# A four-layer graph network on one core: row sums of squares on ScalarE, a third layer with one scale, and another order of loads and of the first product

## The reference

```
x = LN(x + y / max(|y|, 1e-12)),   y = (adj @ x + x) @ w0 + b0
x = LN(x + softmax_like(8 tanh(QK'/ (8 sqrt(128)))) masked by adj, @ x @ v)
x = LN(x + (((si + sj + adj * w_r + g_b) @ x) @ w2 + b2))
x = LN(x + relu(x @ W0 + L x @ W1 + (2 L L - I) x @ W2 + b3))
LN(x) = (x - mean) / sqrt(var + 1e-5)
L = I - dis[:, None] * adj * dis[None, :],   dis = rowsum(adj) ** -0.5
```

## Time and profile before

| | us |
|---|---|
| median of 3 runs (728.14 to 728.96) | 728.53 |
| the profiled execution | 728.63 |
| its span, first to last instruction | 726.5 |
| TensorE busy | 645.3 (89%) |
| VectorE busy | 616.1 (85%) |
| ScalarE busy | 383.5 (53%) |
| GpSimd busy | 72.3 (10%) |

### The profile page before, as it was taken

The page is one execution under the profiler, slowest core; times in us unless marked ns, Lnnn a source line. Parts: engine busy times, 40 slices in busy tenths (PEclk is TensorE's granted clock), DMA queues, the critical chain, the costliest instruction groups (busy, mean ns, idle before and its releaser), DMA issues. The chain is left out here.

```text
span 726.5 us, 17484 instructions
## 1 busy us (share of the span) xinstructions
PE 645.3 (89%) x7478; PEld 488.2 (67%) x7478; DVE 616.1 (85%) x1562; ACT 383.5 (53%) x525; POOL 72.3 (10%) x49
## 2 busy tenths in 40 slices
PE   4937955889999999999999999999999999869894
PEld 3533633456886688667866687668866786638894
DVE  3789898998999899898989899989989897879525
ACT  3928914782359244944467255924494447613402
POOL 0020001000200111002200120011100220020002
PEclk9978996999999999999999999999999999989998
DMA  7100001000100020000200020002000010000102
GB/s 263 45 29 1 1 1 30 0 2 1 31 3 1 2 60 2 1 3 1 60 1 2 1 60 2 1 2 60 2 1 2 5 27 2 1 1 2 31 2 59
DMA packets 20013, 14.54 MB, mean 20 GB/s; under 512 B 864, under 2 KB 18912, under 8 KB 19936
## 3 DMA queue, kind: packets, MB, share of 16 engines
q1 hardware_dynamic: 18816, 12.91, 5.8%
q10 hardware_dynamic: 1120, 0.52, 0.3%
HBM read 9.24 MB, written 4.19 MB: 18 GB/s over the span
## 5 line engine op out<-in xcount | busy, mean ns | idle before, releaser
L240 POOL TENSOR_TENSOR small<-small,minus_half 128x8 f32<-128x8 f32 x39 | 67.9, 1745 | 602.7 <-DVE small L528 479.5
L1215 PE MATMUL av<-vhi,p_hi 128*128 128x129 f16 x512 | 90.1, 221 | 8.8 <-DVE p_lo L776 8.5
L375 ACT ACTIVATE att<-r,coef 128x1024 f32<-128x1024 f32 x64 | 70.4, 1100 | 49.8 <-PE r L1102 49.2
L1218 PE MATMUL av<-vhs,p_lo 128*128 128x129 f16 x512 | 89.9, 220 | 0.0
L1217 PE MATMUL av<-vlo,p_hi 128*128 128x128 f16 x512 | 89.8, 219 | 0.0
L771 DVE TENSOR_TENSOR att<-att,adjT 128x1024 f32<-128x1024 f32 x64 | 78.1, 1221 | 10.9 <-ACT att L377 10.9
L776 DVE SCALAR_TENSOR_TENSOR p_lo<-p_hi,att 128x1024 f16<-128x1024 f16 x64 | 78.1, 1221 | 0.0
L1100 PE MATMUL r<-gr,lap 128*128 128x128 f16 x448 | 75.8, 219 | 0.0
L1102 PE MATMUL r<-gr,lap 128*128 128x128 f16 x448 | 75.8, 219 | 0.0
L1101 PE MATMUL r<-gr,lap 128*128 128x128 f16 x448 | 75.8, 219 | 0.0
L1102 PE MATMUL r<-xq,lap 128*128 128x128 f16 x448 | 75.4, 219 | 0.0
(11 more groups left out here) (300 smaller groups left out, 1924.6 us busy)
## 6 DMA issues: line engine op xcount, KB each, us to landing
x<-in_x SPq DMA_DIRECT2D x8, 512.0 KB, 4.3
lap<-in_adj SPq DMA_DIRECT2D x8, 512.0 KB, 9.4
out<-outb SPq DMA_DIRECT2D x7, 512.0 KB, 3.4
out<-att SPq DMA_DIRECT2D x1, 384.0 KB, 2.8
b_bc<-in_L_gnn_bias SPq DMA_DIRECT2D x3, 64.0 KB, 7.2
x<-in_L_gnn_weight ACTq DMA_DIRECT2D x1, 192.0 KB, 8.1
out<-att SPq DMA_DIRECT2D x1, 128.0 KB, 2.7
x<-in_L_gnn_q ACTq DMA_DIRECT2D x1, 64.0 KB, 3.5
```

Of the source, the lines that this page charges most:

```text
L240: return nc.gpsimd.tensor_tensor(dst, src, minus_half[:], ALU.pow)
L375: nc.scalar.activation(att[:, s], (r1, r0)[t % 2][:], ACT.Tanh, scale=c_tanh).then_inc(S["th"], 1)
L1215: mm(acc, p_hi[:, s, chunk(j)], vhi[:, t, 0:D + 1], start=(t == 0 and j % 3 == 0), stop=False, skip_group_check=True)
L1218: l_ = mm(acc, p_lo[:, s, chunk(j)], vhs[:, t, 0:D + 1], start=False, stop=(t == C - 1), skip_group_check=True)
```

## The change

Row squares: the BATCH_NORM_STATS2 of y and the three operations that combined them are gone. ScalarE runs `row_squares(b, h)`, four Square activations with an accumulator for each half, into the same small tile. In the steady tail half 0 stands behind `y0_half(1)` and ahead of `x3t_hi`, half 1 between `r_hi` and `p_copy`; in steps -1 and 0 both follow `y0_half(1)`.

Third layer: the normalisation of x3 now includes the root of the degree, so the Laplacian of the scaled rows needs only one scale a row, -1/degree. The identity is no longer added: the weights are combined otherwise (w0+w1+w2, w1+4*w2 in place of w1, and w2). The broadcast of dis, its sixteen matmuls and `lap_row` are gone; both parts of a row come straight from adjT, all high parts from ScalarE in the tails of steps -1 and 0, low parts in the attention of steps 0 and 1. The bias is multiplied by the root of the degree (`bias_rows`), and the last normalisation's epsilon by the degree. Scale constants change with it.

`ln_arg` has five operations (norms 0 and 1) or six (2 and 3) in place of seven.

Loads: all of adj ahead of the broadcasts. Opening: y0 is made in eight blocks of 128 columns (`adj_x0_chunk`), one behind the transposes of the next adj block; VectorE makes the adjT copy of blocks 0 and 1; the low part of block 7 is made from PSUM; the first half is projected ahead of the last block; the scales of the weights come in pieces (`weights_max`, `weights_scale`, `weights_split`, `gate_weights`). All row sums of adj follow the squares on ScalarE, and GpSimd takes the row norms' root ahead of the degrees'.

```diff
-LN_ARG = 5
-LN_LINKS = 6
+LN_ARG = (4, 4, 5, 4)
+LN_LINKS = (5, 5, 6, 5)
+DVE_COPIES = 2
...
             for c in range(C):
                 sp.dma_start(adj_rows[:, c, :], adj_v[c]).then_inc(adj_in[c], 16)
-                if c == 1:
-                    for dst, src in ((b0_bc[:], b0), (b2_bc[:], b2), (b3_bc[:], b3.rearrange("a b d -> (a b d)")),
-                                     (wj_bc[:], gw[0:D]), (wi_bc[:], gw[D:2 * D]),
-                                     (wr_gb[:, 0:1], gw[2 * D:2 * D + 1]), (wr_gb[:, 1:2], gb)):
-                        sp.dma_start(dst, src.partition_broadcast(P)).then_inc(S["w_in"], 16)
+            for dst, src in ((b0_bc[:], b0), (b2_bc[:], b2), (b3_bc[:], b3.rearrange("a b d -> (a b d)")),
+                             (wj_bc[:], gw[0:D]), (wi_bc[:], gw[D:2 * D]),
+                             (wr_gb[:, 0:1], gw[2 * D:2 * D + 1]), (wr_gb[:, 1:2], gb)):
+                sp.dma_start(dst, src.partition_broadcast(P)).then_inc(S["bc_in"], 16)
...
+                if nxt:
+                    pool.wait_ge(S["e0_c"], 4 * (i + 2))
+                    inverse_root(small[:, 4, ROOT], small[:, 4, ARG]).then_inc(S["norm_r"], 1)
                 if is_first(i, -1):
                     pool.wait_ge(S["deg_ok"], C)
                     inverse_root(dis[:], deg[:]).then_inc(S["dis_ok"], 1)
-                if nxt:
-                    pool.wait_ge(S["e0_c"], 8 * (i + 2))
-                    inverse_root(small[:, 4, ROOT], small[:, 4, ARG]).then_inc(S["norm_r"], 1)
                 if nxt:
                     norm_root(0, i + 1)
                 if cur:
...
                 copy(a_hi[:, :, chunk(c)], src, ADJ_UP).then_inc(S["adj_hi"], 1)
-                copy(adjT[:, :, chunk(c)], src, LO_UP * P_UP).then_inc(S["adj_cp"], 1)
+                if c == C - 1:
+                    act.wait_ge(S["adj_lo"], C)
+                if c >= DVE_COPIES:
+                    copy(adjT[:, :, chunk(c)], src, LO_UP * P_UP).then_inc(S["adj_cp"], 1)
+                if c == C - 3:
+                    act.wait_ge(S["y0_mm"], 1)
+                    copy(yT[:, 0, half(0)], r1[:, half(0)], Y0_DOWN).then_inc(S["y0_hi"], 1)
...
             def lap_hi_part(*rows):
+                act.wait_ge(S["lap_sc"], 1)
                 for c in rows:
-                    act.wait_ge(S["lap_st"], 2 * (c + 1))
-                    copy(lap[:, 0, c, :], (lap_f, lap_g)[c % 2]).then_inc(S["lap_hi"], 1)
+                    copy(lap[:, 0, c, :], adjT[:, c, :], lap_s[:, c:c + 1]).then_inc(S["lap_hi"], 1)
+
+            def bias_rows():
+
+                act.wait_ge(S["bc_in"], 16 * 7)
+                for c in range(C):
+                    l_ = copy(b3_rows[:, c], b3_bc[:], root_deg[:, c:c + 1])
+                l_.then_inc(S["b3_ok"], 1)
...
+            def row_squares(b, h):
+
+                act.wait_ge(S["e0_c"], 4 * b + 2 + h)
+                for j in range(h * C // 2, (h + 1) * C // 2):
+                    l_ = nc.scalar.activation(tmp[:, j], x1[:, j], ACT.Square, accum_out=small[:, 4, 0, j:j + 1])
+                l_.then_inc(S["norm_sq"], 1)
...
-                if nxt and not is_first(i, 0):
+                if nxt and prev:
                     y0_half(0)
                 if prev:
                     norm(2, i - 1, x3, V_CHUNKS)
+                if nxt:
+                    y0_half(1)
+                    row_squares(i + 1, 0)
+                    if not prev:
+                        row_squares(i + 1, 1)
                 if is_first(i, -1):
-                    degrees(0, 5)
-                if nxt:
-                    y0_half(1)
-                if is_first(i, -1):
-                    degrees(5, C)
+                    degrees(0, C)
+                    lap_hi_part(0, 1)
+                if is_first(i, 0):
+                    lap_hi_part(2, 3, 4, 5, 6, 7)
+                    bias_rows()
...
                         x3t_hi(z_all, i - 1, h)
                     for h in range(2):
                         r_hi(z_all, i - 1, h)
+                    if nxt:
+                        row_squares(i + 1, 1)
                     if last:
                         act.wait_ge(S["q_lo"], 2 * (i - 1))
-                    if is_first(i, 1):
...
             def ln_arg(k_, b, cs=slice(0, C), at=None, before=0):
 
-                ch = Count(dve, S[f"ln{k_}"], b, LN_ARG)
-                ch.base, ch.n = LN_LINKS * b + before, 1
+                ch = Count(dve, S[f"ln{k_}"], b, LN_ARG[k_])
+                ch.base, ch.n = LN_LINKS[k_] * b + before, 1
                 ch.wait()
                 at = k_ if at is None else at
                 st, sm = stats[:, at, cs], small[:, at, :, cs]
                 me, mo = st[:, :, 0, 1], st[:, :, 1, 1]
-                tt(sm[:, 0], me, mo, ALU.add)
-                tt(sm[:, 1], me, mo, ALU.subtract)
-                ch.link(tt(sm[:, 2], st[:, :, 0, 2], st[:, :, 1, 2], ALU.add))
-                tt(sm[:, 3], sm[:, 1], sm[:, 1], ALU.mult)
-                ch.link(ts(sm[:, 4], sm[:, 0], -0.5, None, ALU.mult))
-
-                ch.link(stt(sm[:, 0], sm[:, 3], D / 4.0, sm[:, 2], ALU.mult, ALU.add))
-                ch.mark(ts(sm[:, ARG], sm[:, 0], 1.0 / D, EPS, ALU.mult, ALU.add))
+                tt(sm[:, 0], me, mo, ALU.subtract)
+                ch.mark(stt(sm[:, 2], st[:, :, 0, 2], 0.0 if k_ == 3 else D * EPS, st[:, :, 1, 2], ALU.add, ALU.add))
+                stt(sm[:, 4], me, -1.0, mo, ALU.mult, ALU.subtract)
+                ch.wait()
+                if k_ == 3:
+                    stt(sm[:, 1], sm[:, 0], 0.25, sm[:, 0], ALU.mult, ALU.mult)
+                    ch.link(stt(sm[:, 3], sm[:, 2], 1.0 / D, eps_deg[:, cs], ALU.mult, ALU.add))
+                    ch.mark(tt(sm[:, ARG], sm[:, 3], sm[:, 1], ALU.add))
+                else:
+                    ch.link(stt(sm[:, 1], sm[:, 0], 0.25, sm[:, 0], ALU.mult, ALU.mult))
+                    if k_ == 2:
+                        ch.link(stt(sm[:, 3], sm[:, 2], 1.0 / D, sm[:, 1], ALU.mult, ALU.add))
+                        ch.mark(tt(sm[:, ARG], sm[:, 3], dis2[:, cs], ALU.mult))
+                    else:
+                        ch.mark(stt(sm[:, ARG], sm[:, 2], 1.0 / D, sm[:, 1], ALU.mult, ALU.add))
                 ch.end()
+
+            def shift(sm):
+
+                return stt(sm[:, SHIFT], sm[:, 4], 0.5, sm[:, ROOT], ALU.mult, ALU.mult)
...
+            dve.wait_ge(S["ident_ok"], 3)
+            ts(ident_up[:], ident[:], ADJ_UP, None, ALU.mult).then_inc(S["iu_ok"], 1)
             for c in range(C):
-                dve.wait_ge(S["adj_cp"], c + 1)
-                stt(a_lo[:, :, chunk(c)], adjT[:, :, chunk(c)], ADJ_UP / (LO_UP * P_UP), a_hi[:, :, chunk(c)],
-                    ALU.mult, ALU.subtract).then_inc(S["adj_lo"], 1)
-                if c == C // 2:
+                src = cd((r0[:], r2)[c % 2])
+                if c < DVE_COPIES:
+                    dve.wait_ge(S["adj_hi"], c + 1)
+                    ts(adjT[:, :, chunk(c)], src, LO_UP * P_UP, None, ALU.mult).then_inc(S["adj_cv"], 1)
+                    dve.wait_ge(S["adj_cv"], c + 1)
+                if c == C - 1:
+                    dve.wait_ge(S["adj_hi"], C)
+                    l_ = stt(a_lo[:, :, chunk(c)], src, ADJ_UP, a_hi[:, :, chunk(c)], ALU.mult, ALU.subtract)
+                else:
+                    if c >= DVE_COPIES:
+                        dve.wait_ge(S["adj_cp"], c + 1 - DVE_COPIES)
+                    l_ = stt(a_lo[:, :, chunk(c)], adjT[:, :, chunk(c)], ADJ_UP / (LO_UP * P_UP), a_hi[:, :, chunk(c)],
+                             ALU.mult, ALU.subtract)
+                l_.then_inc(S["adj_lo"], 1)
+                if c == 1:
                     weights_max()
-                if c == 0:
-                    dve.wait_ge(S["ident_ok"], 3)
-                    ts(ident_up[:], ident[:], ADJ_UP, None, ALU.mult).then_inc(S["adj_lo"], 1)
-            weights()
...
+                if c == 5:
+                    dve.wait_ge(S["y0_hi"], 1)
+                    stt(yT[:, 1, half(0)], r1[:, half(0)], Y0_DOWN, yT[:, 0, half(0)], ALU.mult, ALU.subtract).then_inc(S["y0_lo"], 1)
+
+            def lap_scales():
+
+                dve.wait_ge(S["dis_ok"], 1)
+                tt(dis2[:], dis[:], dis[:], ALU.mult)
+                stt(lap_s[:], dis[:], -LAP_UP / (LO_UP * P_UP), dis[:], ALU.mult, ALU.mult)
+                ts(eps_deg[:], deg[:], EPS, None, ALU.mult)
+                tt(root_deg[:], deg[:], dis[:], ALU.mult).then_inc(S["lap_sc"], 1)
 
             def lap_lo_part(*rows):
                 for c in rows:
                     dve.wait_ge(S["lap_hi"], c + 1)
-                    tt(lap[:, 1, c, :], (lap_f, lap_g)[c % 2], lap[:, 0, c, :], ALU.subtract).then_inc(S["lap_lo"], 1)
+                    stt(lap[:, 1, c, :], adjT[:, c, :], lap_s[:, c:c + 1], lap[:, 0, c, :],
+                        ALU.mult, ALU.subtract).then_inc(S["lap_lo"], 1)
...
-                stt(z.u[:], cd(r2), c_u, row(b3_bc[:]), ALU.mult, ALU.add).then_inc(S["u_ok"], 1)
```

(88 more changed lines are left out.)

148 lines of the change are left out of this document (56 added, 92 removed).

## The result

The changed kernel takes 724.64 us (median of 4 runs, 723.78 to 725.29) against 728.46 (4 runs, 728.14 to 728.96): ratio 0.9943, with the interval 0.993 to 0.9957. Its profiled execution took 725.29 us with a span of 723.1, 3.4 less than before.

What follows compares the result with a forecast made beforehand. TensorE was taken to bound the steady period, and chains through VectorE, GpSimd and ScalarE the opening and first tail. From 728.63 us, +3.5 + 2.1 - 1.75 - 1.5 = +2.4 gave 731.0 us, range 725.5 to 736.

Steps and rivals of the forecast that it cites:

- the opening: Start up to the first scores: earlier y, but later x1 root and slower clock, together +2.1 us (0 to +4).
- The first two batches: First tail and batch 1's attention, plus work ahead of the first mask: less VectorE work, together -1.75 us (-3 to 0).
- The Squares in six tails: Tails of batches 1 to 6: Square activations on ScalarE make TensorE late, 0.6 us a batch, +3.5 us in all.
- Rival B: Steady tails: Squares at 0.24 us each, TensorE's lateness equals its old wait; 727.5 us, no change; chance 0.25.
- D: Steady tails: Squares at 0.51 us each, +12.5 us instead of +3.5, 740 us; chance 0.06.
- E: Steady tails: table changes around each group of Squares, some 5 us a batch, 761 us; chance 0.02.
- Rival C: Opening: TensorE reaches its fast clock before block 0, opening 0.9 us shorter; with hidden Squares 724.5 us; chance 0.17.
- wrong if 78.6 or less: Steady tail: a period of about 79.2 us was expected; 78.6 or less would show the forecast wrong.
- wrong if before 61: Opening: first scores were expected near 63.4 us; a start before 61 would show the forecast wrong.
- The end: End of the kernel, without Squares: six shorter norm arguments one behind another on VectorE's chain, -1.5 us.

Runs made afterwards that it cites:

- doubled Squares: The changed kernel with two of the first four Square activations done twice in the six steady tails, second results unread: 731.01 us, ratio 1.0035.
- the run with 48 and 44 products: The changed kernel with unread TensorE products added, 48 in the opening and 44 in the first batch's tail: 725.27 us, ratio 0.9955.

## Why the prediction was wrong

The sign was wrong because two terms of the sum were too large, each by one step: the Squares by some 2.9 us and the opening by 1.5. The first two batches came out 1.1 lower than forecast as well, mostly by the clock.

**The Squares in six tails: +3.5 forecast, +0.54 over five periods measured.** The mechanism was right. TensorE's product is 1.04 late (1.12 forecast), the Laplacian 1.29 (1.52), the wait for x1 is gone, and x1 is no longer last. Two sizes were off. First, a group of four takes 1.16 us, not 1.3: Squares start 0.29 apart. I had taken the length from 0.81 ns a column (0.32, where it is 0.30), and rounded four times 0.31 up. The estimate worked out from the Trainium skill ("ScalarE: Activation LUTs", section "What ACT_TABLE_LOAD costs"), 0.20 for the activation and with the read 0.29 each, 1.2 us a group, stood in the prediction and was the better one; the trace agrees with it, with 0.29 measured. That it makes the forecast 0.5 us a batch lower doesn't follow, though: two groups of 1.16 for 1.3 take off 0.28. Second, the slack: I took the 0.97 that the row of the transposes names as idle. This counts from the modelled end of the last matmul, 0.22 after its start, while back-to-back matmuls start 0.056 apart. From start to start the trace of before has

```profile
429.07 0.22 PE L1102 MATMUL r<-gr,lap 128*128 128x128 f16 x1
430.26 0.44 PE L1106 MATMUL r<-ident,x 128*128 128x128 f32 x2 [0.97 <-DVE x L545]
```

1.19 us, that is 1.13 more than back to back. With 1.29 late and 1.13 covered 0.16 remain, where the forecast had 1.52 - 0.97 = 0.55 and rounded it to 0.6. The period is longer by 0.11 us. A difference of two almost equal numbers needs both to a tenth. The doubled Squares show the other side of the same edge: with the slack used up, 0.58 us more are 0.58 us more a period.

Rival B, hidden Squares, was the nearer case for this term. I had argued against it from the presence of the accumulator read (0.19), which is there and costs what the 0.29 includes. Rivals D and E didn't happen. The trace has one table load of 1.283 us, as before, though Square isn't among the functions that the Trainium skill ("ScalarE: Activation LUTs", section "Table sets: the hidden batching unit") names.

**Rival C, 724.5, has the measured number, but not by its way.** It wanted the opening 0.9 us shorter, with the degrees done before 48; in the profiled execution the opening is 0.58 longer and the degrees end at 49.2. In the runs whose block 0 ran at the fast clock its first step is there, with the first root 1.6 us earlier, not 3. The period (78.72, wrong if 78.6 or less) and the first scores (61.79, wrong if before 61) gave neither of the signs that I had set for being wrong: the miss is spread over terms that no sign watched.

**The opening: +2.1 forecast, +0.58 measured.** The chain came out as worked out: second half of y at 38.83 (39.2 forecast), degrees done at 49.2 (49.5), argument of x1 at 47.5 (47.8), its root at 50.88 (51.3), transposes at 54.18 (54.6). The transposes are 0.47 later than before, where +1.0 was forecast. The step that failed is the clock: +1.1 because the sixteen matmuls of the diagonal are gone. From transposes to scores it takes 7.61, and took 7.50 with them. Those matmuls ended 4.74 us before the transposes, and in an experiment the clock fell behind a pause of 2.53. Other profiles bear it out: the two variants of the kernel before, which have these matmuls too, take 7.93 (the Squares alone) and 7.99 (the short arguments alone), and those of the changed kernel without them and without products in their place take 7.36 to 8.82. What I had read as their effect, 7.50 against 8.79 in the next tail, is within what this stretch differs by from one execution to the next. The opening as a whole depends on the execution too: the run with 48 and 44 products had the early one, and its transposes of x1 start at 52.57, 1.14 us earlier than before the change instead of 0.47 later.

**The first two batches: -1.75 forecast, -2.89 measured.** The work terms nearly hold: from the first scores to the next root of row norms -1.17 (-0.9 forecast), in the argument behind it -0.37 (-0.36), and the wait for low parts in batch 1 fell by 0.5 (0.55 forecast). The step that was missing is the clock of the profiled execution of before in the first tail: from transposes to scores it took 8.79 us there against 7.89, 0.90 of the difference. The Squares alone and the short arguments alone, without an edit to this place, take 7.65 and 7.56, so the 8.79 belongs to that execution and not to the kernel. It also ran at the slow level for some 3.4 us in the first attention, where the changed kernel has 1.00:

```profile
70.00:74.00 4.00, 3.89 (x30) 2.19 (x31) 3.61 (x4) 3.97 (x5) 0.00 (x0) 0.68 0.00 0
74.00:76.00 2.00, 2.00 (x26) 1.89 (x26) 0.49 (x1) 1.97 (x3) 0.00 (x0) 0.78 0.00 0
```

This cost nothing: the short arguments alone had 1.00 there and need 44.69 us from the first scores to the next root, where the kernel before needs 44.70. About a microsecond up or down is also the spread of the runs of the kernel before (727.62 to 729.57).

**The end: -1.5 forecast, -1.59 measured**, by five or six operations of 0.08 to 0.2 us each where there were seven. That it agrees to 0.1 is partly luck. From GpSimd's root at 670.49 (667.85 after the change) to the last one 0.72 are gained, and this part is the same within 0.02 us in all profiles of the changed kernel's variants. But ahead of it, from the root at 575.73 on, the run with 48 and 44 products takes 0.97 us more than the changed kernel for the same instructions. The Squares alone, without an edit there, takes 0.76 more than the kernel before from the root at 638.84 on.

What I had underrated as a whole is the short argument. It stood in my sum as -1.5 at the end and as 0.36 inside the tail's balance, which the Squares ate. Alone it is worth 5.0 us, more than the whole change. The changed kernel without its Squares gains 7.1, so the new third layer and opening together bring some 2 us more, which no run separates. Of this the Squares' place and the root order take back some; moved by a few instructions, these two are worth a further 8.6.

## What to carry to other kernels

When work is moved to an idle engine, look at the place in that engine's queue before its length: the same four Squares cost 1 us a batch more ahead of a copy that TensorE waits for than behind it. Take the slack of TensorE from start to start of its matmuls, not from the idle time in brackets, and where a forecast is the difference of a delay and a slack, let its sign stay open within the error of both. A wait for something that isn't needed yet (the degrees) doesn't belong ahead of a step on the chain in an engine that works in order. And before a difference between two stretches of one trace is put down to a cause, look at the same stretch in a second execution.
